# Graph attention in two layers: which source blocks the DMA transposes and which TensorE does

## The reference

```python
def transformer_conv(x, src, dst, Wq, bq, Wk, bk, Wv, bv, Ws, bs, H, C, concat):
    q = (x @ Wq + bq).reshape(n, H, C); k = (x @ Wk + bk)...; v = (x @ Wv + bv)...
    alpha = jnp.einsum('ehc,ehc->eh', q[dst], k[src]) / jnp.sqrt(C)
    amax = segment_max(alpha, dst)
    p = jnp.exp(alpha - amax[dst])
    denom = segment_sum(p, dst) + 1e-16
    out = segment_sum(p[:, :, None] * v[src], dst) / denom[:, :, None]
    out = out.reshape(n, H * C) if concat else out.mean(axis=1)
    return out + x @ Ws + bs
h = relu(transformer_conv(x, ..., H=4, C=128, concat=True))     # layer 1
out = transformer_conv(h, ..., H=2, C=128, concat=False)        # layer 2
return layernorm(x + out)
```

## Time and profile before

| what | value |
|---|---|
| median of three executions | 1883.69 us (1883.66 to 1884.6) |
| the profiled execution | 1881.96 us |
| its span, first to last instruction | 1879.6 us |
| busy: PE, DVE, ACT, POOL | 1782.6, 1511.0, 1252.5, 1135.4 us (95%, 80%, 67%, 60% of the span) |
| mean granted clock of TensorE | 0.978 of full speed |
| transposing DMAs of `flipped` | 600 |

### The profile page before, as it was taken

The page is one execution under the profiler, slowest core; times in us unless marked ns, Lnnn a source line. Parts: engine busy times, 40 slices in busy tenths (PEclk is TensorE's granted clock), DMA queues, the critical chain, the costliest instruction groups (busy, mean ns, idle before and its releaser), DMA issues. The chain is left out here.

```text
span 1879.6 us, 44239 instructions
## 1 busy us (share of the span) xinstructions
PE 1782.6 (95%) x14656; PEld 1339.7 (71%) x14656; DVE 1511.0 (80%) x4506; ACT 1252.5 (67%) x2088; POOL 1135.4 (60%) x1432
## 2 busy tenths in 40 slices
PE   3779889999999999999999999989899999999997
PEld 3556557777777777777777777756577777777876
DVE  6999878888888788888888888723788888988886
ACT  4578867777777677777777777711366666767675
POOL 4200056777777777777677776713367676766765
PEclk9789999999999999999999999989999999999999
DMA  6688958877888887888788887680488899999985
GB/s 163 171 233 239 244 119 156 157 151 150 160 157 157 147 154 154 158 156 155 152 157 152 159 156 151 116 228 1 95 168 176 173 180 178 174 183 180 176 178 108
DMA packets 753648, 301.70 MB, mean 161 GB/s; under 512 B 655853, under 2 KB 734065, under 8 KB 750171
## 3 DMA queue, kind: packets, MB, share of 16 engines
q1 hardware_dynamic: 752252, 296.96, 78.7%
q0 software_dynamic: 640, 1.63, 0.3%
q10 hardware_dynamic: 528, 0.26, 0.1%
HBM read 93.62 MB, written 47.83 MB: 75 GB/s over the span
## 5 line engine op out<-in xcount | busy, mean ns | idle before, releaser
L1393 POOL TENSOR_TENSOR prob_parts_l<-prob_l,prob_parts_l 125x512 f16<-125x512 f32 x600 | 721.2, 1232 | 14.8 <-ACT prob_parts_l L1480 14.8
L1471 ACT ACTIVATE prob_l<-prob_l,neg_max_l 125x1024 f32<-125x1024 f32 (+1 forms) x450 | 521.7, 1161 | 4.7 <-DVE neg_max_l L1555 4.7
L1725 PE MATMUL score_l<-room,QT_l 128*128 128x512 f16 (+2 forms) x2100 | 512.5, 354 | 0.3 <-POOL QT_l L1383 0.3
L1486 ACT CAST probT_l<-transposed_l 128x375 f16<-128x375 f32 x450 | 212.9, 473 | 433.0 <-PE transposed_l L1749 433.0
L1755 PE MATMUL output_l<-V,prob_flipped_l 128*128 128x256 f16 x2400 | 459.4, 272 | 3.4 <-DMA prob_flipped_l<-prob_parts_l 3.4
L1757 PE MATMUL output_l<-V,prob_flipped_l 128*128 128x128 f16 x2400 | 427.5, 219 | 0.0
L1547 DVE CUSTOM_DVE_ANT_0 prob_l<-score_l,mask_even 125x512 f32<-125x512 f32 (+2 forms) x546 | 334.1, 616 | 112.4 <-PE score_l L1725 111.5
L1547 DVE CUSTOM_DVE_ANT_0 prob_l<-score_l,mask_odd 125x512 f32<-125x512 f32 (+2 forms) x504 | 309.2, 615 | 107.1 <-PE score_l L1725 106.5
L1480 ACT CAST prob_parts_l<-prob_l 125x1024 f16<-125x1024 f32 x300 | 309.5, 1033 | 0.1
L1755 PE MATMUL output_l<-V,probT_l 128*128 128x256 f16 x1350 | 273.2, 274 | 2.7 <-DVE probT_l L1560 1.6
L1755 PEld LDWEIGHTS output_l<-V,prob_flipped_l 128*128 128x128 f16 x2400 | 233.7, 97 | 55.1 <-issue 5.1
(11 more groups left out here) (195 smaller groups left out, 2380.4 us busy)
## 6 DMA issues: line engine op xcount, KB each, us to landing
mask_scratch<-log SPq DMA_DIRECT2D x87, 420.0 KB
mask_even<-mask_scratch SPq DMA_DIRECT2D x25, 448.0 KB
mask_odd<-mask_scratch SPq DMA_DIRECT2D x24, 448.0 KB
mask_odd<-mask_scratch SPq DMA_DIRECT2D x12, 896.0 KB
mask_even<-mask_scratch SPq DMA_DIRECT2D x12, 896.0 KB
prob_flipped_l<-prob_parts_l SPq DMA_TRANSPOSE x600, 3.2
hT_scratch<-rowsT_l SPq DMA_DIRECT2D x24, 250.0 KB, 3.9
mask_odd<-mask_scratch SPq DMA_DIRECT2D x12, 471.2 KB
```

Of the source, the lines that this page charges most:

```text
L1393: pool.tensor_tensor(parts[0:TP, 1, a:b], prob[:, h % 2, a:b], parts[0:TP, 0, a:b], ALU.subtract).then_inc(s_flo, 1)
L1471: act.activation(e, e, ACT.Exp, bias=neg_max[:, h % 2:h % 2 + 1], accum_out=total[:, h % 2, c:c + 1]).then_inc(s_exp, 1)
L1486: act.copy(probT[:, q, 0, 0:n, 0:TP], flipped_in_psum(h, q, n)).then_inc(s_hi, 1)
L1725: last = pe.matmul(score_bank(h, p)[:, 0:b - a], QT[:, h % 2, i, :], KT[:, h, j, a:b], start=n == 0, stop=n == len(products) - 1)
```

## The change

In layer 1 the pieces are cut anew (`CUTS1`: 512, 512, 512, 384, 384, 512 and 309 columns), and ND becomes 5: the DMA transposes five pieces, 18 blocks, and TensorE two, of 4 and 3 blocks. The second part of the exponentials grows from 1024 to 1280 columns, the third shrinks from 1077 to 821. Layer 2 keeps its cuts. The slots are written with ND: for ND = 4 they give the order of before, for ND = 5 TensorE has two flipped pieces of step s-1 left over, in slots 0 and 1, `values` begins in slot 3 and not 2, and DVE's `value_sum` stands in slot 2 and not 1. Layer 2's `v_back` is formed at the start of `projections2` by two DVE instructions from V's scale, and no longer beside layer 1's second tile.

```diff
-FB = 16
 CUTS = ((0, 512), (512, 1024), (1024, 1536), (1536, 2048), (2048, 2432), (2432, 2816), (2816, N))
-HALVES = ((0, 1), (2, 3))
-ND = 4
-NQ = len(CUTS) - ND
-EXP_PARTS = ((0, 1), (2, 3), (4, 5, 6))
+CUTS1 = ((0, 512), (512, 1024), (1024, 1536), (1536, 1920), (1920, 2304), (2304, 2816), (2816, N))
+DMA_PIECES = {1: 5, 2: 4}
...
-STEPS2 = 12
+STEPS2 = 11
...
                 link(dve.memset(V[:, NT - 1, :, :, :], 0.0))
+                v_back = L["v_back"]
+                link(dve.tensor_scalar(v_back[:, :].bitcast(I32), up[:, 2, :].bitcast(I32), -1, INVERSE, ALU.mult, ALU.add))
+                link(dve.tensor_scalar(v_back[:, :], v_back[:, :], 1.0 / P_UP, None, ALU.mult))
                 dve.wait_ge(s_colp, 1)
...
+    CUTS_OF = CUTS1 if layer == 1 else CUTS
+    ND = DMA_PIECES[layer]
+    NQ = NP - ND
+    HALVES = ((0, 1), tuple(range(2, ND)))
+    EXP_PARTS = HALVES + (tuple(range(ND, NP)),)
...
-                    if n == 11:
-                        dve.tensor_scalar(back, back, 1.0 / (V_UP * P_UP), None, ALU.mult).then_inc(s_chain2, 1)
...
                         for k in range(NP):
-                            if k == 1 and not (is_first(t) and h == 0):
+                            if k == ND - 3 and not (is_first(t) and h == 0):
                                 value_sum(s - 1, (h - 1) % H)
...
                             if k < NQ:
                                 transposes(s, h, k)
-                            if k == 0 and not (is_first(t) and h == 0):
-                                flipped_values(s - 1, (h - 1) % H, ND - 1)
-                            if 2 <= k <= NQ + 1:
-                                values(s, h, k - 2)
-                            if k >= NP - ND + 1:
-                                flipped_values(s, h, k - (NP - ND + 1))
+                            if k < ND - 3 and not (is_first(t) and h == 0):
+                                flipped_values(s - 1, (h - 1) % H, 3 + k)
+                            if ND - 2 <= k < ND - 2 + NQ:
+                                values(s, h, k - (ND - 2))
+                            if k >= 4:
+                                flipped_values(s, h, k - 4)
...
-                flipped_values(NT * H - 1, H - 1, ND - 1)
+                for p in range(3, ND):
+                    flipped_values(NT * H - 1, H - 1, p)
```

More of the change, by code:

```diff
@@ L137, in build @@
             "rows": sb("scale_rows2", [C, 3, H2 * C]),
-            "v_back": sb("v_back2", [C, H2 * C]),
             "cols": sb("bias_cols2", [C, 2, H2]),
@@ L176, in build @@
                 "V": sb2("V2", [C, NT, H2, 2, C], F16),
-                "v_back": second["v_back"],
+                "v_back": sb2("v_back2", [C, H2 * C]),
                 "Wq": second["W"][1],
@@ L864, in _ @@
                 dve.wait_ge(s_row, 16 * len(ROW_SPLIT))
-                for a, b in CUTS:
+                for a, b in CUTS1:
                     dve.scalar_tensor_tensor(first_mask[:, a:b], first_mask[:, a:b], STEEP, first_mask[:, a:b],
@@ L1207, in attention @@
               mask=None, s_cleared=None):
-    v_back2 = second and second["v_back"]
     featT, KT, V, v_back, Wq, Ws, bq = (L[n] for n in ("featT", "KT", "V", "v_back", "Wq", "Ws", "bq"))
     W = H * C if layer == 1 else C
+    CUTS_OF = CUTS1 if layer == 1 else CUTS
[3 more added lines that the diff above has]
+    EXP_PARTS = HALVES + (tuple(range(ND, NP)),)
+    FB = CUTS_OF[ND][0] // C
+    QB = max(len(blocks_in(cut)) for cut in CUTS_OF[ND:])
     with ExitStack() as ctx:
@@ L1227, in attention @@
         flipped = sb("prob_flipped", [C, 2, 2, FB, C], F16)
-        probT = sb("probT", [C, NQ, 2, 3, C], F16)
+        probT = sb("probT", [C, NQ, 2, QB, C], F16)
         skip = sb("skip", [TP, W])
@@ L1266, in attention @@
         PART_PIECES = ((0, 1), (2, 3), (4, 5), (6,)) if layer == 1 else ((0, 1, 2, 3), (4, 5, 6))
-        MASK_PARTS = [(CUTS[pieces[0]][0], CUTS[pieces[-1]][1]) for pieces in PART_PIECES]
+        MASK_PARTS = [(CUTS_OF[pieces[0]][0], CUTS_OF[pieces[-1]][1]) for pieces in PART_PIECES]
         CLEAR_AT = ({(0, 2): 0, (0, 5): 1, (1, 2): 2, (1, 5): 3, (2, 1): 4, (2, 4): 5, (2, 6): 6} if layer == 1 else
@@ L1305, in half_cols @@
         def half_cols(half):
-            return CUTS[HALVES[half][0]][0], CUTS[HALVES[half][-1]][1]
+            return CUTS_OF[HALVES[half][0]][0], CUTS_OF[HALVES[half][-1]][1]
         with nc.Block() as block:
@@ L1387, in low_parts @@
                     for p in range(ND):
-                        a, b = CUTS[p]
+                        a, b = CUTS_OF[p]
                         half = half_of(p)
@@ L1469, in exponentials @@
                         act.wait_ge(s_max, s + 1)
[L1470 removed]
+                    e = prob[:, h % 2, CUTS_OF[EXP_PARTS[c][0]][0]:CUTS_OF[EXP_PARTS[c][-1]][1]]
                     act.activation(e, e, ACT.Exp, bias=neg_max[:, h % 2:h % 2 + 1],
@@ L1482, in high_part @@
                 def high_part(s, h, q):
-                    n = len(blocks_in(CUTS[ND + q]))
+                    n = len(blocks_in(CUTS_OF[ND + q]))
                     act.wait_ge(s_tp, NQ * s + q + 1)
@@ L1618, in scale_step @@
                     if n == 8:
-                        power(back, v).then_inc(s_chain2, 1)
+                        power(v, v).then_inc(s_chain2, 1)
                     if n == 9:
-                        inverse(v, back).then_inc(s_chain2, 1)
+                        inverse(v, v).then_inc(s_chain2, 1)
                     if n == 10:
                         dve.tensor_scalar(v, v, V_UP, None, ALU.mult).then_inc(s_chain2, 1)
-                    if n == 11:
-                        dve.tensor_scalar(back, back, 1.0 / (V_UP * P_UP), None, ALU.mult).then_inc(s_chain2, 1)
                 def row_norm(t, step):
@@ L1746, in transposes @@
                     pe.wait_ge(s_exp, EP * (s + 1))
-                    for i, b in enumerate(blocks_in(CUTS[ND + q])):
+                    for i, b in enumerate(blocks_in(CUTS_OF[ND + q])):
                         w = width_of(b)
@@ L1771, in flipped_values @@
                         pe.wait_ge(s_flip[half][n], 16 * (s + 1))
-                    for b in blocks_in(CUTS[p]):
+                    for b in blocks_in(CUTS_OF[p]):
                         hi, lo = (flipped[:, h % 2, n, b, :] for n in range(2))
```

2 lines of the change are left out of this document (1 added, 1 removed).

## The result

The changed kernel takes 1922.98 us (median of 4 runs, 1918.76 to 1923.09) against 1883.68 for the kernel before on the same chip (4 runs, 1882.29 to 1884.6): a ratio of 1.0204 with a 95% interval of 1.0186 to 1.0221. It is slower, by 39.3 us.

A forecast was written before the change was run, and what follows sets the result against it. Layer 1 was taken as bound by TensorE, 9.78 us a step. Per tile 3.15 waits less 0.86 transposes and 0.17 old wait, +2.12; 25 tiles +53.0, with small terms +49.6: 1933 us predicted, range 1910 to 1960.

The forecast's parts named there:

- head 3: Layer 1, head 3: a long clearing ahead delays the first low difference to 1.42 us; TensorE waits 0.64 us.
- DMA waits: TensorE's waits on the transposing DMAs, 3.4 us in the whole program, should vanish: -3.4, bounds -3.4 to 0.
- The chain: DVE's instructions per layer 1 step up to emptying `O`: bank ready 3.91 us after the first transpose, wanted at 3.44.
- The waits by head: Layer 1, TensorE ahead of `values`: waits of 0.47, 1.07, 0.97 and 0.64 us, 3.15 per tile.
- Head 2's clearing: Layer 1, DVE: clearing 384 mask columns now precedes the emptying, adding 0.50 us; 0 to 0.8 more, taken as 0.
- v_back: Layer 2, start of projections: two DVE instructions, at most 1.1 us, ahead of a 1.59 us wait; cost 0, at worst 1.1.
- Head 1's old wait: Layer 1, head 1: TensorE's present wait for the emptying, 0.17 us per tile, subtracted from the new waits.
- The end of layer 1: One more flipped piece left over and its low part later: 0 to 1 us, taken as 0.5.
- in time: Rival: the emptying of `O` in layer 1 starts early enough, kernel faster by 29 us, 1854 us; chance 0.09.
- nearly in time: Rival: chain shorter by 0.5 us in each head, waits 1.18 per tile, 1885 us, no change; chance 0.03.
- The clock: Rival: four waits per tile make TensorE's clock drop, 85 us if once per tile, 2018 us; chance 0.03.
- The low half comes late: Rival: second part's low half, via POOL and a ten-block DMA, adds 0.59 us per step, 59 us: 1992; chance 0.03.

The follow-up runs named there:

- e3: Changed kernel, in layer 1 the emptying of `O` moved early into DVE's slot 1 and the skip addition behind the second low difference; 1871.87 us, ratio 0.9942.
- e6: e3's kernel, in layer 1 ACT scales the query ahead of its first copy into the high part; 1859.53 us, ratio 0.9869.
- e5: Kernel before with only layer 2's `v_back` formed by two DVE instructions at the start of its projections, scale chain one instruction shorter; 1883.62 us, ratio 1.0001.
- e1: Changed kernel, in layer 1 only the emptying of `O` moved from slot 2 to slot 1, ahead of the second low difference; 1885.03 us, ratio 1.0012.
- e7: e6's kernel, in layer 1 `skip_product` moved from slot 6 of head 0 to slot 0 of head 1; 1851.40 us, ratio 0.9831.

## Why the prediction was right

The mechanism and the sign hold, and the size nearly: 1933 us was forecast, 1922.98 came, 39.3 us of loss instead of 49. The time lies just under 1924, the lower end of the range worked out from rows; the end at 1910, lowered for a chain sized wrongly, covers it. Three terms make most of the difference: head 3 (5 us less), an old wait that vanished and that the sum did not count (`skip_product`, 5.6 less) and the DMA waits (2.4 more). Point by point:

- **The chain.** Predicted from the first transpose of a step: first low difference 1.25, emptying 3.16, `values` 3.91 us, while TensorE wants at 3.44. Medians over all tiles in head 0: 1.24, 3.13, 3.88 and 3.44.
- **The waits by head.** Predicted 0.47, 1.07, 0.97, 0.64; measured by starts 0.44, 1.04, 1.03, 0.44. Per tile 2.95 instead of 3.15. These are medians; added up step by step the waits are 76 us, where some 78 were forecast.
- **Head 3 is the term that was mis-sized.** I carried over that the first low difference comes late there because a long clearing stands ahead of it. In the changed kernel it comes at 1.24 us, as in the others, because this clearing, of 309 columns, takes 0.89 us in the median and not 1.30. Its length goes with POOL's work. Here is the POOL instruction that was under way when the clearing of the earlier trace rows began, at 634.46:

```profile
634.30 1.15 POOL L1393 TENSOR_TENSOR prob_parts_l<-prob_l,prob_parts_l 125x512 f16<-125x512 f32 x1
```

  It ends at 635.45 and the clearing at 635.79, 0.34 us later. The same pair in the changed kernel, in e3 and in e6:

```profile
609.12 1.16 POOL L1400 TENSOR_TENSOR prob_parts_l<-prob_l,prob_parts_l 125x512 f16<-125x512 f32 x1
609.73 0.89 DVE L1540 SCALAR_TENSOR_TENSOR mask_odd<-mask_odd 125x309 f32<-125x309 f32 x1
```
```profile
670.42 1.16 POOL L1400 TENSOR_TENSOR prob_parts_l<-prob_l,prob_parts_l 125x512 f16<-125x512 f32 x1
670.54 1.38 DVE L1540 SCALAR_TENSOR_TENSOR mask_odd<-mask_odd 125x309 f32<-125x309 f32 x1
```
```profile
665.04 1.16 POOL L1400 TENSOR_TENSOR prob_parts_l<-prob_l,prob_parts_l 125x512 f16<-125x512 f32 x1
665.65 0.88 DVE L1543 SCALAR_TENSOR_TENSOR mask_odd<-mask_odd 125x309 f32<-125x309 f32 x1
```

  Each time the clearing ends 0.33 to 0.34 us after POOL's piece; what differs is how much of the piece was left. TensorE's wait in head 2 is not needed for the short clearing: e3 and e6 both lack that wait, DVE begins the clearing 0.45 us ahead of the first transpose in both, as in the changed kernel, and the first difference comes at 1.47 us in e3 and at 1.24 in e6, whose edit lets POOL begin its low parts earlier. Price of the error: 25 x 0.2 = 5 us.
- **Head 2's clearing.** I took no more than before and kept 0.8 for the bounds. It takes 0.67 us, 0.59 up to the next start, against 0.57 and 0.50. The Trainium skill (SBUF — State Buffer, Who interferes with whom) would have let it wait for one POOL piece, up to 1.2 us. The trace agrees with the rule: the piece under way when this clearing began, at 644.96 in the rows above, had 0.25 us left, and the clearing ends 0.42 us behind it.

```profile
644.30 0.91 POOL L1400 TENSOR_TENSOR prob_parts_l<-prob_l,prob_parts_l 125x384 f16<-125x384 f32 x1
```

- **Not foreseen: `skip_product`.** Before, TensorE waits at the end of head 0 for ACT's copy, between 400 and 1000 us 15 times:

```profile
PEld skip_rows_l L1735 <- ACT rowsT_l L1465: 3.6, 15, 0.2
```

  In the changed kernel TensorE arrives later and the row is gone. By starts it was 0.22 us a tile, 5.6 in all. I had not looked for old waits that a new one swallows, beyond head 1's.
- **DMA waits.** Predicted to vanish (-3.4), measured 3.4 to 2.4 (-1).
- **`v_back`**: nothing, as e5 shows.

The profiled executions differ by 41.07 us. Waits: 25 x 2.95 less the first step's 0.45, +73.3. Transposes: -21.5. Head 1's old wait: -4.2. `skip_product`: -5.6. DMAs: -1.0. Sum +41.0. That it meets the measured figure to 0.1 us is chance: with the waits added up step by step (76) it would be some 44, and from the first transposes of layer 1's first step to those of its last the two executions differ by 38.2 us; the rest lies outside, where the executions profiled here vary by 2 to 4 us. The end of layer 1, predicted at +0.5, is not to be told apart in this.

The rivals: "in time" and "nearly in time" fell with the first PE timeline. The clock stayed at 1.00 through a wait of 0.44 to 1.04 us in every step, so short holes after each group did not let it fall; the Trainium skill's tale of an oscillating clock (TensorE: Matmul & The Clock Gate, A second HAM failure mode) is not borne out here. "The low half comes late" did not decide the changed kernel, but it was right about what is next: e1 and e3 pay waits on the flipped blocks as soon as the emptying is out of the way (14.8 and 13.4 us, where that rival had 59), and e6 takes most of them back.

What stays open: how much of e6's gain is the earlier cast on POOL and how much the later first high part, since one edit moves both.

## What to carry to other kernels

When work on the bound engine is made shorter, look at what stands between its two uses of a single buffer, and work out the other engine's chain up to the emptying from a common start: here 0.22 us saved per step was paid with 0.74. Before an instruction's length is carried over from one place to another, look at what another engine was doing beside it. A slot that is written with a constant of the tiling (`k == ND - 3`) moves other work along with it; place the emptying by what it must follow and precede. And sum the waits that a new wait hides: old ones go, and the next ones appear when it is removed.

## What the runs showed of the hardware that was not expected

A long clearing of the mask on DVE is one that begins while POOL is at work and ends just behind it. In layer 1 of the kernel before, without its first and last tile, 93 of 161 clearings took over 0.1 us more than their undisturbed length. In all 93 a POOL instruction was under way at the start, and the clearing ended at a fixed time after that instruction: 0.34 us for 309 columns, 0.42 for 384, 0.55 for 512, each within 0.01 us and 0.13 to 0.14 short of the undisturbed lengths of 0.48, 0.55 and 0.68. In the changed kernel this holds for all 64 such clearings. So beside POOL's low parts the length of a clearing follows from when it begins.

A DMA transpose that carries the low halves takes longer from issue to landing with ten blocks than with eight: 3.42 us in the median against 3.08 in layer 1 of the changed kernel. For the high halves, which are issued ahead of them, the medians do not differ (3.82 for ten, 3.85 for eight). Single transfers took up to 5.3 to 5.7 us between 700 and 800 us (changed kernel, e3 and e7). The median over all of them went from 3.2 us before to 3.5; the row of the changed kernel (issues, us to landing):

```profile
prob_flipped_l<-prob_parts_l SPq DMA_TRANSPOSE x600, 3.5
```

It is 3.5 in e7 too, which waits 4.7 us for them in the whole program: the longer way does not by itself make TensorE wait.
